# Third layer: nine buffers for the weights of blocks, three of them over the scattered rows, and a new order of all engines

## What is computed

```
xn = _layernorm(x, axis=-1)
x = x + _L2_attn_ref(xn, ...) + _L2_ffn_ref(xn, ...)

# _L2_attn_ref: a selective scan over time, 256 channels, 16 states
xz = x @ W_in;  xc, z = jnp.split(xz, 2, axis=-1)
xc = silu(causal convolution of 4 taps of xc, + conv_b)
x_dbl = xc @ W_x                      # dt_raw, B_mat (16), C_mat (16)
dt = softplus(dt_raw @ W_dt + b_dt);  A = -exp(A_log)
def step(h, inp):
    dA = jnp.exp(dt_t[..., None] * A)
    h = dA * h + dt_t[..., None] * B_t[:, None, :] * x_t[..., None]
    y = jnp.einsum('bds,bs->bd', h, C_t)
y = (y + D_param * xc) * silu(z);  return y @ W_out

# _L2_ffn_ref: 14 experts of width 256, the best two of each token
probs = softmax(x @ gate_w.T);  top2_p, top2_i = top_k(probs, 2)
w = top2_p / top2_p.sum(-1)
hh = gelu(einsum('nd,edf->nef', x, w1) + b1)
all_out = einsum('nef,efd->ned', hh, w2) + b2
result = clip(x + w0 * all_out[top2_i[0]] + w1 * all_out[top2_i[1]], -100, 100)
```

## Time and profile before

| what | us |
|---|---|
| time, median of 3 runs (1758.12 to 1763.32) | 1758.94 |
| time of the profiled execution | 1759.55 |
| its span | 1757.6 |

### The profile page before, as it was taken

How to read it: one execution, slowest core, us unless ns; L and a number is a source line. 1 busy time by engine, 2 the same in 40 slices (tenths; PEclk the granted TensorE clock), 3 DMA queues, 4 the chain that set the end, 5 groups by cost and what they waited for, 6 DMA issues and landing times. The chain is left out here.

```text
span 1757.6 us, 19878 instructions
## 1 busy us (share of the span) xinstructions
PE 1571.4 (89%) x6998; PEld 682.6 (39%) x7006; DVE 1246.5 (71%) x1752; ACT 1154.2 (66%) x1608; POOL 234.7 (13%) x230
## 2 busy tenths in 40 slices
PE   6999999999999999997999899999656677668998
PEld 3333333333333333332444466663224344333675
DVE  5977777777777777761343338776897889966997
ACT  5788888888888888885524387335636645523773
POOL 1001111111111011121000100000580000284000
PEclk9999999999999999999999899998887788877999
DMA  6200101010000000001142121113344656531000
GB/s 209 45 13 1 31 7 25 13 25 12 25 12 21 16 1 13 7 1 58 36 90 70 26 63 50 39 37 89 128 135 146 199 166 196 183 108 38 1 1 25
DMA packets 66571, 103.64 MB, mean 59 GB/s; under 512 B 8999, under 2 KB 32518, under 8 KB 66452
## 3 DMA queue, kind: packets, MB, share of 16 engines
q1 hardware_dynamic: 64426, 98.18, 19.4%
q0 software_dynamic: 2048, 4.20, 0.8%
HBM read 86.39 MB, written 15.87 MB: 58 GB/s over the span
## 5 line engine op out<-in xcount | busy, mean ns | idle before, releaser
L708 DVE TENSOR_REDUCE best<-quad 128x2 f32<-128x1024 f32 x256 | 309.9, 1222 | 130.3 <-PE quad L498 127.9
L622 ACT ACTIVATE weights<-quad 128x1024 f32<-128x1024 f32 x256 | 255.7, 1029 | 28.6 <-PE quad L523 28.3
L2617 PE MATMUL quad<-l_st,ident 128*128 128x512 f32 x256 | 144.8, 713 | 52.7 <-DVE l_st L2932 52.7
L540 PE MATMUL quad<-weights,values 128*32 128x512 f32 x1024 | 136.4, 605 | 0.4 <-ACT weights L622 0.4
L110 PE MATMUL quad<-q,wf 128*128 128x512 f32 x256 | 121.5, 606 | 0.7 <-DVE mk L679 0.3
L110 PE MATMUL quad<-hid,wf 128*128 128x512 f32 x256 | 116.6, 599 | 0.0
L2915 DVE TENSOR_TENSOR l_st<-l_u,l_bs 128x1024 f32<-128x1024 f32 x64 | 76.7, 1219 | 42.9 <-PE quad L2617 29.0
L2617 PEld LDWEIGHTS quad<-l_st,ident 128*128 128x128 f32 x256 | 56.2, 233 | 120.4 <-DVE l_st L2932 63.4
L566 ACT ACTIVATE hid<-quad,col 128x512 f32<-128x512 f32 x128 | 84.9, 688 | 21.4 <-PE quad L110 21.3
L110 PE MATMUL quad<-sq_all,mean_w 128*128 128x512 f32 x176 | 94.5, 636 | 1.9 <-ACT sq_all L1367 0.9
L498 PE MATMUL quad<-ks,qs 48*128 48x512 bf16 x512 | 89.5, 385 | 6.8 <-DVE best L708 6.3
(11 more groups left out here) (448 smaller groups left out, 3033.3 us busy)
## 6 DMA issues: line engine op xcount, KB each, us to landing
l_bs<-xd_dram SPq DMA_DIRECT2D x32, 512.0 KB
l_c_rows<-xd_dram SPq DMA_DIRECT2D x32, 512.0 KB
l_weights<-in_F_w SPq DMA_DIRECT2D x45, 257.0 KB, 3.4
end_cs<-comb SPq DMA_DIRECT2D x32, 256.0 KB, 3.7
l_cs<-comb SPq DMA_DIRECT2D x32, 256.0 KB, 3.6
wf<-in_L_f SPq DMA_DIRECT2D x16, 256.0 KB, 2.6
qs<-q_dram SPq DMA_DIRECT2D x16, 192.0 KB, 3.4
ks<-k_dram SPq DMA_DIRECT2D x16, 192.0 KB, 4.3
```

The lines of the kernel that those rows point to most:

```text
L540: last = nc.tensor.matmul(out[32 * j:32 * j + 32, :], values[:, kt, GH * g + j, :], weights[p % BUFS][:, j % 2, j // 2, :], start=(kt == 0 ...
L622: nc.scalar.activation(weights[p % BUFS][:, slot, :, :].rearrange("p a t -> p (a t)"), doubles.of("weigh", m, i), ACT.Exp, scale=scale).th ...
L708: nc.vector.tensor_reduce(heads[:, :, slot, qt, c], doubles.of("search", m, i).rearrange("p (a t) -> p a t", a=2), AX.X, ALU.max).then_inc ...
L2617: last = nc.tensor.matmul(y[d][:, c:c + BANK], core.ident[:, :], st[n % RING][:, c:c + BANK], start=False, stop=(s == NS - 1), skip_group_ ...
```

## The change

The table PLAN_2 is another one, for all engines. Two of its lines show the form (the numbers themselves tell a reader little):

```diff
-    "turned": (56, 57, 65, 66, 83, 84, 99, 110, 114, 116, 129, 132,),
+    "turned": (61, 62, 65, 76, 77, 87, 92, 99, 100, 107, 110, 117,),
-    "join": (135, 141, 222, 223,),
+    "join": (184, 219, 222, 223,),
```

The weights of blocks get nine buffers. The six of before stay; three more lie over the token rows, and SyncE waits for the whole scatter before it loads the first of them:

```diff
-    RING, KEPT_WEIGHTS = 4, 6
+    RING, KEPT_WEIGHTS, OWN_WEIGHTS = 4, 9, 6
...
-        kept = sb("weights", [P, KEPT_WEIGHTS * W])
-        weights = [kept[:, i * W:(i + 1) * W] for i in range(KEPT_WEIGHTS)]
+        kept = sb("weights", [P, OWN_WEIGHTS * W])
         rows = sb("rows", [P, TILES, D])
+        rows_flat = rows[:, :, :].rearrange("p t d -> p (t d)")
+        weights = [kept[:, i * W:(i + 1) * W] for i in range(OWN_WEIGHTS)] + [rows_flat[:, i * W:(i + 1) * W] for i in range(KEPT_WEIGHTS - OWN_WEIGHTS)]
...
                         if b == 0:
                             sp.wait_ge(blocks.known, 1)
+                        if b == OWN_WEIGHTS:
+                            sp.wait_ge(scattered, 16 * 2 * TILES)
                         if b >= KEPT_WEIGHTS:
                             sp.wait_ge(made, (b - KEPT_WEIGHTS) // 4 + 1)
```

More of the change, by code:

```diff
@@ L2186 @@
 PLAN_2 = {
[L2187 to L2196, removed]
-    "turned": (56, 57, 65, 66, 83, 84, 99, 110, 114, 116, 129, 132,),
-    "hidden": (60, 61, 62, 69, 74, 78, 79, 82, 90, 92, 96, 100, 107, 108, 113, 118, 123, 125, 130, 131, 137, 139, 140,),
@@ L2199 @@
[L2199 to L2205, removed]
@@ L2206 @@
-    "slots": (24, 27, 28, 29, 32, 37, 55, 59, 66, 75, 89, 101,),
-    "store": (42, 48, 78, 79, 87, 97, 102, 113, 114, 123, 126, 127,),
-    "comb": (88, 131,),
+    "var": (3, 6, 7, 8,),
+    "x": (9, 10, 11, 12, 20, 21, 22, 23,),
+    "z": (14, 15, 16, 47, 18, 19, 37, 46,),
+    "xd": (25, 26, 35, 36,),
+    "dt": (27, 28, 30, 31, 45, 48, 49, 58,),
+    "out": (133, 153, 163, 164,),
+    "logits": (13,),
+    "ranks": (24,),
+    "turn": (34,),
+    "rows": (17, 29, 32, 33,),
+    "turned": (61, 62, 65, 76, 77, 87, 92, 99, 100, 107, 110, 117,),
@@ new lines @@
+    "hidden": (63, 64, 66, 67, 74, 75, 79, 80, 85, 86, 93, 94, 97, 98, 105, 106, 111, 113, 118, 121, 126, 127, 130,),
+    "made": (68, 69, 78, 88, 89, 101, 102, 112, 120, 125, 131, 132,),
+    "sum": (146, 149, 150, 158,),
+    "st": (2, 30,),
+    "b_row": (5, 6, 7, 8, 16, 18, 19, 22, 23, 26, 35, 41, 47, 59, 62, 74, 80, 88, 96, 102, 106, 107, 116, 117, 122, 123, 126, 127, 131, 133, 134, 137,),
+    "c_row": (3, 4, 14, 15, 17, 20, 21, 24, 25, 37, 42, 50, 54, 64, 65, 81, 87, 97, 103, 105, 110, 114, 118, 121, 124, 125, 128, 130, 132, 135, 136,
+        138,),
@@ L2209 @@
+    "weights": (10, 11, 12, 13, 31, 32, 33, 34, 39, 40, 44, 45, 46, 48, 49, 52, 56, 57, 58, 60, 61, 66, 67, 68, 69, 70, 71, 72, 75, 84, 85, 86, 89,
+        90, 91, 93, 94, 98, 99, 100, 101, 104, 108, 109, 111,),
+    "slots": (27, 28, 29, 36, 38, 51, 53, 73, 76, 78, 82, 83,),
+    "store": (43, 55, 63, 77, 79, 92, 95, 112, 113, 115, 119, 120,),
+    "comb": (9, 129,),
     "scatter": (2, 3, 4, 5, 6, 7, 8, 9, 10, 11, 12, 13, 14, 15, 16, 17, 18, 19, 20, 21, 22, 23, 24, 25, 26, 27, 28, 29, 30, 31, 32, 33,),
-    "gather": (34, 35, 36, 37, 38, 39, 40, 41, 42, 43, 44, 45, 46, 47, 48, 49, 50, 51, 52, 53, 54, 55, 57, 58, 59, 60, 61, 62, 63, 64, 65, 66,),
@@ L2211 @@
-    "clip": (56, 68, 70, 72,),
+    "gather": (34, 35, 36, 37, 38, 39, 40, 41, 42, 43, 44, 45, 46, 47, 48, 49, 50, 51, 52, 53, 54, 55, 56, 57, 58, 59, 60, 61, 62, 63, 64, 65,),
+    "clip": (66, 68, 70, 72,),
     "join_experts": (67, 69, 71, 73,),
[L2213 to L2247, removed]
@@ new lines @@
+    "gate_z": (14, 15, 18, 60, 20, 21, 49, 71,),
+    "silu": (16, 17, 41, 42,),
+    "copy_xd": (27, 29, 45, 46,),
+    "lin": (28, 30, 33, 34, 57, 58, 62, 72,),
+    "abs": (31, 36, 64, 89,),
+    "exp": (32, 38, 65, 105,),
+    "ln": (35, 40, 66, 108,),
+    "exp_a": (12,),
+    "decay": (43, 47, 48, 50, 51, 52, 53, 54, 55, 56, 59, 61, 63, 67, 68, 69, 70, 73, 74, 77, 84, 85, 86, 88, 90, 96, 97, 98, 106, 107, 109, 111,
+        121, 122, 123, 129, 130, 133, 134, 135, 137, 138, 143, 144, 148, 149, 152, 153, 154, 155, 160, 161, 162, 164, 167, 178, 179, 181, 189, 190,
+        191, 192, 193, 196,),
@@ L2260 @@
+    "gate": (125, 126, 220, 221,),
+    "join": (184, 219, 222, 223,),
+    "route": (8, 10,),
+    "number": (11,),
+    "copy_turn": (17,),
+    "weigh": (80,),
 }
```

41 lines of the change are left out of this document (30 added, 11 removed).

## The result

The changed kernel takes 1716.23 us in the median of 4 runs (1713.85 to 1717.53), the kernel before beside it 1760.04 (4 runs, 1758.12 to 1763.32). The ratio is 0.9748, 95% interval 0.9728 to 0.9767: 43.8 us faster. Forecast were 34.5 us, 1724.5 in a range from 1710 to 1745. The profiled execution took 1713.85 us, its span is 1712.1 (before 1757.6).

A forecast was written before the change was run, and what follows sets the result against it. The third layer was taken as bound by VectorE's work plus idle time. Idle -32, start -2.5 and tail 0 gave -34.5 us: 1725.05 for the profiled execution, 1724.5 for the median, range 1710 to 1745.

The forecast's parts named there:

- the start: Before the third layer's first scan: routing ahead of the second half's convolutions takes 2.5 us off idle time.
- idle time between first scan and last product: VectorE in the third layer: 50.0 us of idle time become 18, so -32.
- the tail: After the last product with C: GpSimd's later additions stay hidden behind VectorE's last join; 0 us, bounds 0 and 5.
- First slots: TensorE's first turning of expert slots: the 9.59 us wait goes, 3 us left for the block behind it.
- Weights and rows: Expert stage, nine weight buffers: waits for TensorE's state sums fall to 7 us, for rows of B and C to 4.
- Density: Turns 16 to 39: TensorE's 89 us fit VectorE's 118; DMA fits with 230 GB/s at about 0.77 share.
- Rival (a): Packed expert stretch: SyncE and DMA fall behind, late weights reach VectorE, 19 us more: 1743; chance 0.15.
- rival (c): Packed expert stretch: TensorE becomes the bound at low clock, deciding under 0.59; 1784 us; chance 0.05.
- Gather: Late third layer: waits of 6.72 and 7.69 us go; third quarter just in time, 2 us left, bounds 0 and 15.
- rival (b): Gather's third quarter late: ScalarE's scalings hold decays, VectorE stops at the scan; 12 us more, 1736; chance 0.12.

The follow-up runs named there:

- changed again: The changed kernel measured a second time with no edit, against the kernel before: 1719.39 us, ratio 0.9756.
- both locks removed: Changed kernel with turn 63's decay ahead of third-quarter scalings, TensorE's third and fourth gathered-row sums later, VectorE's second join earlier: 1712.73 us, again 1707.66.
- fourth sum behind outputs: Kernel of 1712.73 us with TensorE's third gathered-row sum two additions later and its fourth behind the last products with w_out: 1720.99 us, ratio 0.9763.
- fourth sum between: Kernel of 1712.73 us with TensorE's fourth gathered-row sum behind turn 63's last addition, ahead of the last two products with w_out: 1711.18 us.
- sums late, old order: Kernel before with decays of turns 59 to 63 ahead of the gathered-row scalings and TensorE's four sums further behind: 1759.66 us, ratio 0.9984.
- the end in the old order: Changed kernel with the steps from turn 44 on in the kernel before's order on TensorE, ScalarE, VectorE and SyncE: 1710.74 us, ratio 0.973.

## Why the prediction was right, and where its sizes were off

**Right as a whole.** By the profiled executions the layer lost 45.2 us, forecast were 34.5 in the same terms: the start 4.0 (2.5), idle time between first scan and last product 37.8 (32), VectorE's work 1.8 (0), the tail 1.7 (0).

**Start.** The scatter starts at 1234.76 (near 1235 forecast), the first scan 53.13 us into the layer instead of 57.15. How much of the 4.0 is the order's stays open: in profiles with the old start order the time from VectorE's first instruction of the layer to its first scan was 54.4, 52.6 and 50.1 us, with the new one 49.5 to 51.8.

**First slots.** The wait of 9.59 went, as said, and the 3 us left for it are 0. By itself the earlier scatter gave nothing, as the early routing in the old order shows, where the first scan came 7.7 us later; it pays only where the first scan isn't held.

**Weights and rows.** 7 us were left for TensorE's sums (L2617, now L2621) and 4 for the rows; ahead of the gather nothing of either remains, beside it 2.4 us for the sums. This is the term that made the gain larger than forecast (together with the slots 14 us forecast, under 1 measured ahead of the gather). The mechanism was half right: nine buffers in the old order show that six cost most through SyncE's queue of rows (7.2 of the 8.4 us in that profile), while VectorE's waits for TensorE stayed as they were. Of the 44 us the buffers alone gave 11. The early routing alone gave nothing, and with the old order of the end nothing was lost. The other 33 come from the new order of the start and the middle together with the buffers: one buffer less costs 12, and a late numbering 7, through the bank that it holds. The new order with six buffers was not run, so order and buffers are not told apart further.

**Density.** The count held: 230 GB/s at a share of 0.77 forecast, 233 at 0.77 measured. From the product with C of turn 15 to that of turn 39 (1321.74 to 1441.47) 119.7 us passed, where 118 were counted. TensorE was busy 100.5 of them at a granted clock of 0.91; that is by estimate 91 us at the full clock, where 89 were counted. Rival (a) and rival (c) (it needed a clock under 0.59) are out in this order; (a) is what eight buffers do.

**Gather.** Here the step failed by its size. Its 2 us of idle time are 7.69 + 1.63, at the place and by the lock of rival (b) (a scan waits for a decay behind a scaling, then TensorE's third sum). The prediction counts from the end of the product with C of turn 39, which is at 1441.47:

```profile
1440.25 1.22 DVE L2936 TENSOR_TENSOR l_st<-l_st,l_c_rows 128x1024 f32<-128x1024 f32 x1
```

From there its sum ran +10 for the gather's start, 53 for 24 gathers, 2 to land. Measured are +14.4, 62.7 and 1.7. The gather starts 9.7 us behind the last output on TensorE (1446.20), where the sum took 3.6 from before: its copy ends at 1448.8, and its store lands 7 us later. VectorE's own count held: it stood ready for the scan of turn 57 at +72.6, where +70.5 was counted. The decay, counted for +67, was done at +80.2. The duration 1.91 + 0.30 came from the scatters; those of the first 24 gathers are 0.94 to 6.42. Rival (b)'s "worst duration shown", 3.01, was the worst of its rows and not of the trace: one gather of the kernel before took 4.28 us. The text also had the gather start "some 40 us" earlier in layer time; it is 72 (328.3 to 255.8), because the 40 counted the turns moved and left out the idle time removed ahead of it (2.7 + 9.6 + 18.0 before 1524).

**What ends the layer** was only half in the prediction: besides VectorE's last join, GpSimd's last join of gathered rows can hold the next layer back, by the rule in the last section. In the changed kernel's profile the two bounds lie 0.6 us apart (1571.3 and 1571.9), so the tail forecast as 0 held with little room. The rule also explains why removing waits at the end won so little.

The sentence that the prediction draws from the Trainium skill on tensor_tensor is answered in the last section.

## What to carry to other kernels

A wait behind a slow producer (here the gather) shows wherever the first consumer stands in a queue; moving the consumers back mostly moves the wait (0 us won in the old order, 5 to 10 in the new), so follow the producer's chain to the end of the layer before counting any wait as gain. When buffers are scarce, look at what else stands in the queue that loads them: the other transfers behind the blocked one may be what costs. And where a step is moved, ask which bank or queue it held for the others: holding the numbering back cost 7 us in one order, and bringing the routing forward gave nothing in the other.

## What the runs showed of the hardware

**GpSimd's end costs 6.7 us.** In all 14 profiles the next layer's first VectorE instruction came within 0.1 us of the later of two times: 1.5 us behind the end of VectorE's last join, or 6.7 behind that of GpSimd's (the later one in five of them). Seven of them, worked out from the timelines (us):

| kernel | gather, start to end | GpSimd's join ends, +6.7 | VectorE's join ends, +1.5 | next layer |
|---|---|---|---|---|
| before | 1527.7 to 1589.1, 61.4 | 1612.0 | 1616.5 | 1616.5 |
| changed | 1455.8 to 1531.1, 75.3 | 1571.3 | 1571.9 | 1571.9 |
| changed again | 1470.5 to 1542.3, 71.8 | 1583.9 | 1581.7 | 1584.0 |
| both locks removed, second time | 1456.9 to 1541.5, 84.6 | 1562.5 | 1562.8 | 1562.7 |
| fourth sum behind outputs | 1459.9 to 1541.7, 81.8 | 1578.1 | 1573.6 | 1578.1 |
| fourth sum between | 1454.7 to 1547.9, 93.2 | 1564.8 | 1560.4 | 1564.9 |
| sums late, old order | 1535.4 to 1598.8, 63.3 | 1619.5 | 1615.1 | 1619.5 |

So where a layer ends on GpSimd and VectorE, GpSimd's last work should end 5 us ahead of VectorE's. Between the layers the program clears semaphores and has all engines meet; what GpSimd does in the 6.7 us no row shows.

**The same 32 gathers take 61 to 95 us.** In the new order the gather is the longer the fewer waits VectorE has beside it: 72 to 77 us with 9 to 17 us of waits between 1455 and 1545 (5 profiles), 82 to 95 with 1 to 5 (5 profiles). This suggests that a part of each wait removed was given back; but the same kernel, with both locks removed and few waits both times, took 94.5 and 84.6 us, so one profile doesn't tell how much. The durations of all indirect DMAs sorted by what VectorE did meanwhile (before, then changed): standing still 0.95 and 0.95 us in the mean, only tensor_tensor forms 1.81 and 1.53, only scans 2.12 and 1.73, both 1.90 and 2.70. The Trainium skill, "SBUF — State Buffer", section "Who interferes with whom", infers that a tensor_tensor leaves descriptor generation alone; the trace disagrees, with 1.81 and 1.53 us beside tensor_tensor forms alone against 0.95, and scans slow the DMA as well. The rows show the whole duration of the instruction, not which part of its work is slowed. Why some gathers take 4.1 to 7.6 us, with hardly one in the old order (4.28 us in three of its four profiles), stays open: "sums late, old order" has few waits beside its gather, and 63 us.

**The best version** of those run is the changed kernel with both locks removed, 1712.73 and 1707.66 us in two measurements. The fourth sum between (1711.18) and the end in the old order (1710.74) can't be told from it.
